# Causal mask of two attention stages: from mask products on TensorE to a minimum on VectorE

## What is computed

```python
scores = jnp.einsum('bhqk,bhsk->bhqs', q, k) / jnp.sqrt(jnp.float32(dk))
causal_mask = jnp.triu(jnp.ones((s, s), dtype=bool), k=1)
scores = jnp.where(causal_mask, jnp.float32(-1000000000.0), scores)
weights = jax.nn.softmax(scores, axis=-1)
...
num = jnp.exp(jnp.einsum('bhqd,bhkd->bhqk', q_rot, k_rot) * scale)
den = jnp.sum(jnp.exp(jnp.einsum('bhqd,bhkd->bhqk', q, k) * scale), axis=-1, keepdims=True)
attn = num / den
causal = jnp.tril(jnp.ones((C, C), dtype=bool))
attn = jnp.where(causal[None, None], attn, 0.0)
```

## Time and profile before

| | us |
|---|---|
| median of 3 runs | 5669.14 |
| lowest, highest run | 5666.31, 5673.63 |
| profiled execution, its own time | 5685.95 |
| its span in the trace | 5684.2 |

### The profile page before, as it was taken

How to read it: one execution, slowest core, us unless ns; L and a number is a source line. 1 busy time by engine, 2 the same in 40 slices (tenths; PEclk the granted TensorE clock), 3 DMA queues, 4 the chain that set the end, 5 groups by cost and what they waited for, 6 DMA issues and landing times. The chain is left out here.

```text
span 5684.2 us, 145095 instructions
## 1 busy us (share of the span) xinstructions
PE 5317.8 (94%) x51344; PEld 3675.0 (65%) x51344; DVE 3822.2 (67%) x7798; ACT 3092.0 (54%) x4722; POOL 3094.0 (54%) x1917
## 2 busy tenths in 40 slices
PE   8988967699999999999978799999999999989889
PEld 6655645377777777777755377777777777756556
DVE  2343246578877887788756487788778877855545
ACT  3343323366666666666645366666666666642542
POOL 0000014578777877787720477787778777820200
PEclk9989977799999999999979799999999999999899
DMA  1000000111111111111100111111111111110000
GB/s 41 4 1 32 1 7 2 48 37 51 45 52 44 47 49 52 44 44 52 41 15 1 38 42 52 44 47 49 52 44 43 52 43 53 36 44 1 7 23 8
DMA packets 110452, 197.68 MB, mean 35 GB/s; under 512 B 21408, under 2 KB 28848, under 8 KB 110256
## 3 DMA queue, kind: packets, MB, share of 16 engines
q1 hardware_dynamic: 110256, 194.99, 12.1%
HBM read 53.29 MB, written 1.05 MB: 10 GB/s over the span
## 5 line engine op out<-in xcount | busy, mean ns | idle before, releaser
L2660 POOL TENSOR_TENSOR stage_qk<-stage_halves 128x1024 f32<-128x1024 f32 x384 | 906.2, 2360 | 683.9 <-DVE stage_halves L2742 683.9
L2671 POOL TENSOR_TENSOR stage_rnorm<-stage_clamped,minus_half 128x16 f32<-128x16 f32 x384 | 1116.5, 2908 | 31.9
L2678 POOL TENSOR_TENSOR stage_qk<-stage_qk,stage_rnorm 128x1024 f32<-128x1024 f32 x384 | 731.2, 1904 | 15.4
L2532 ACT ACTIVATE stage_qkT<-stage_turn 128x512 f32<-128x512 f32 x768 | 457.2, 595 | 416.1 <-PE stage_turn L2270 408.0
L2512 ACT ACTIVATE stage_square<-stage_wide 128x1024 f32<-128x1024 f32 x384 | 393.5, 1025 | 417.7 <-PE stage_wide L2253 417.7
L2322 PEld LDWEIGHTS stage_pv<-stage_v_win,stage_probsT 96*64 96x64 f32 x12288 | 421.4, 137 | 303.6 <-issue 271.4
L2544 ACT ACTIVATE stage_probsT<-stage_flip 96x512 f32<-96x512 f32 x768 | 450.3, 586 | 208.6 <-PE stage_flip L2308 208.6
L2322 PE MATMUL stage_pv<-stage_v_win,stage_probsT 96*64 96x65 f32 x12288 | 528.0, 228 | 10.1 <-ACT stage_probsT L2544 8.8
L2739 DVE TENSOR_TENSOR stage_halves<-stage_wide,stage_tables 128x1024 f32<-128x1024 f32 x384 | 470.0, 1224 | 70.4 <-issue 38.0
L2742 DVE TENSOR_TENSOR stage_halves<-stage_wide,stage_tables 128x512 f32<-128x512 f32 x768 | 490.6, 680 | 0.0
L2270 PE MATMUL stage_turn<-ident,stage_qk 128*128 128x128 f32 x3072 | 478.3, 278 | 7.9 <-POOL stage_qk L2678 6.5
(11 more groups left out here) (295 smaller groups left out, 9759.7 us busy)
## 6 DMA issues: line engine op xcount, KB each, us to landing
stage_v_win<-stage_v SPq DMA_DIRECT2D x384, 195.0 KB, 2.6
stage_v_win<-stage_v SPq DMA_DIRECT2D x384, 130.0 KB, 2.4
stage_v_win<-stage_v SPq DMA_DIRECT2D x192, 65.0 KB, 2.2
stage_wq<-in_T_wq SPq DMA_DIRECT2D x12, 512.0 KB, 4.2
stage_wk<-in_T_wk SPq DMA_DIRECT2D x12, 512.0 KB, 3.4
stage_wv<-in_T_wv SPq DMA_DIRECT2D x12, 512.0 KB, 3.5
stage_wo<-in_T_wo SPq DMA_DIRECT2D x12, 512.0 KB, 3.5
stage_w_up<-in_L_w_up SPq DMA_DIRECT2D x8, 512.0 KB, 6.9
```

The lines of the kernel that those rows point to most:

```text
L2532: nc.scalar.activation(target, tiles4(turn), ACT.Copy).then_inc(att["qkT"], 1)
L2660: nc.gpsimd.tensor_tensor(qk[:, n, :], halves[:, n % 2, 0, :], halves[:, n % 2, 1, :], ALU.add)\
L2671: nc.gpsimd.tensor_tensor(rnorm[:, n, :], clamped[:, n, :], chip.minus_half[:, :].to_broadcast([P, LH]), ALU.pow)\
L2678: nc.gpsimd.tensor_tensor(heads, heads, rnorm[:, n, :].rearrange("p (h o) -> p h o", o=1).to_broadcast([P, LH, LD]), ALU.mult).then_inc(at ...
```

## The change

The eight pairs of mask products of each sample go, in level 0 and in level 3; `maskT` goes with them. The exponential is now taken of unmasked scores. For each pair VectorE takes a minimum (`keep_past`) of the diagonal blocks, 128 x 512 elements of two heads and two blocks, with a triangle `limits` that is 0 where the key is later than the query and the largest float elsewhere. `weigh` waits for the new signal `kept`, not for `probs`. The masks of level 0's `first_score` stay. `limits` adds 64 KB to each pack that the stage loads, and the load of the masks shrinks by 32 KB.

```diff
 def attention_signals(level):
...
+    if level != 2:
+        per.update(kept=PAIRS)
...
+    usable = "kept" if causal else "probs"
...
+        diagonals = probs[:, :, :].rearrange("p h (b s) -> p h b s", s=P)[:, :, 0:3:2, :]
...
-                if causal:
-                    for side in range(2):
-                        nc.tensor.matmul(kinds2(duo[:, side, :])[:, :, 0:P], ident_bf[:, :],
-                                         maskT[:, :].rearrange("p (o s) -> p o s", o=1).to_broadcast([P, T, P]),
-                                         start=True, stop=False, skip_group_check=True)
...
-                                               query[:, first:SEQ], start=not causal, stop=True, skip_group_check=True)
+                                               query[:, first:SEQ], start=True, stop=True, skip_group_check=True)
...
-                pe.wait_ge(*sig("probs", step, 2 * g + 2))
+                pe.wait_ge(*sig(usable, step, 2 * g + 2))
...
+            def keep_past(step, n):
+
+                dve.wait_ge(*sig("probs", step, n + 1))
+                own = diagonals[:, 2 * n:2 * n + 2]
+                limits = tiles["limits"].rearrange("p (h t s) -> p h t s", h=1, t=1).to_broadcast([P, 2, T, P])
+                nc.vector.tensor_tensor(own, own, limits, ALU.min).then_inc(sig["kept"], 1)
...
                 if runs(s - 1):
                     reduce(s - 1, 3)
+                if causal and runs(s - 2):
+                    keep_past(s - 2, 5)
...
+                if causal and runs(s - 2):
+                    keep_past(s - 2, 6)
                 if runs(s):
                     reduce(s, 0)
+                if causal and runs(s - 2):
+                    keep_past(s - 2, 7)
+                if causal and runs(s - 1):
+                    keep_past(s - 1, 0)
                 if runs(s - 2):
                     divide(s - 2, 0)
...
                 if runs(s):
                     reduce(s, 1)
+                if causal and runs(s - 1):
+                    keep_past(s - 1, 1)
                 if runs(s - 2):
                     divide(s - 2, 1)
+                if causal and runs(s - 1):
+                    keep_past(s - 1, 2)
...
                 if runs(s + 1):
                     copy_v(s + 1)
+                if causal and runs(s - 1):
+                    keep_past(s - 1, 3)
                 if not softmax and runs(s + 1):
                     rotate(s + 1)
                 if runs(s):
                     reduce(s, 2)
+                if causal and runs(s - 1):
+                    keep_past(s - 1, 4)
```

More of the change, by code:

```diff
@@ L791 @@
 _last = [("bo", D), ("wo", D)]
-ATTN_PARTS = {0: _every + _softmax + _last, 2: [("gamma", 1), ("beta", 1)] + _every + _softmax + _last,
-              3: _every + [("wq_swap", D), ("wk_swap", D), ("rope", 2 * SEQ)] + _last}
+ATTN_PARTS = {0: _every + _softmax + [("limits", P)] + _last, 2: [("gamma", 1), ("beta", 1)] + _every + _softmax + _last,
+              3: _every + [("wq_swap", D), ("wk_swap", D), ("rope", 2 * SEQ), ("limits", P)] + _last}
 def attention_signals(level):
@@ L825, in stage_attention @@
             tiles["rope"] = tiles["rope"].rearrange("p (n s) -> p n s", n=2)
-        masks = sb("masks", [P, 3 * P], BF16)
-        ident_bf, mask, maskT = (masks[:, n * P:(n + 1) * P] for n in range(3))
+        masks = sb("masks", [P, 2 * P], BF16)
+        ident_bf, mask = (masks[:, n * P:(n + 1) * P] for n in range(2))
         wq, wk, wv, wo, bo = (tiles[n] for n in ("wq", "wk", "wv", "wo", "bo"))
@@ L2982, in attention_layout @@
     above = np.triu(np.full((P, P), MASKED, np.float32), 1)
-    a["mask"], a["maskT"] = above.astype(bf16), np.ascontiguousarray(above.T).astype(bf16)
+    a["mask"] = above.astype(bf16)
     pairs = np.arange(D) ^ 1
@@ L3015, in attention_layout @@
     a["A3_rope"] = np.stack([np.tile(t, HEADS).astype(np.float32).T for t in tables], axis=1)
+    a["A0_limits"] = a["A3_limits"] = np.where(above.T < 0, 0.0, np.finfo(np.float32).max).astype(np.float32)
     for level, parts in ATTN_PARTS.items():
         a[f"A{level}_pack"] = joined(a, f"A{level}_", parts)
-    a["masks"] = np.concatenate([a["ident_bf"], a.pop("mask"), a.pop("maskT")], axis=1)
+    a["masks"] = np.concatenate([a["ident_bf"], a.pop("mask")], axis=1)
     del a["heads_of"], a["aug_of"]
```

## The result

The changed kernel is slower: a median of 5720.76 us (5703.44 to 5723.12, 4 runs) against 5671.39 us (5666.31 to 5673.67, 4 runs) for the kernel before on the same chip, ratio 1.0082 with a 95% interval of 1.0060 to 1.0103. That is 49 us by the medians and 47 by the ratio; I had forecast 17, in a range up to 5706. The profiled execution took 5722.89 us (span 5721.1), 36.9 us above that of before; the profiled execution of before was itself 14.6 us above its median.

A forecast was written before the change was run, and what follows sets the result against it. TensorE was busy for 94% of the span, and hand-written order within each stage was taken to count. Level 0 -13, level 3's order +11.5 and clock +18 gave +16.5 on 5669.1: 5686 us, range 5664 to 5706.

The forecast's parts named there:

- Mask products, 0.32 us each: TensorE, levels 0 and 3: each removed mask pair saves 0.32 us, 64 pairs at most 20.5 us per stage.
- Level 0, 13 us gained: Level 0: 20.5 us of masks less 4.7 for waits at `weigh` 3 and 2 for statistics; bounds 6 and 18.
- 2 us for the statistics: VectorE, level 0: statistics between pair 4's minimum and the maxima's reduction cost at most 1.07 us in two or three samples.
- Level 3, the stop: TensorE waits 3.1 us at `weigh` 3 because pair 7's minimum stands behind `reduce(s,0)`; a sample takes 26.34 us, not 24.03.
- Only pair 3's minimum in level 3 falls into such a product ... so I count 0.69 for all: VectorE: every minimum takes 0.69 us, upper end 1.02, though pair 3's in level 3 runs beside GpSimd's key product.
- The clock, 18 us: Level 3: TensorE's stops bring two half-clock stretches per sample, 3.26 us in each of six samples, less one existing fall.
- the walk: Level 3: one changed sample followed piece by piece from `weigh` 3 to `weigh` 3, 2.31 us lost, 13.9 in six samples.
- the ends: Level 3's two stage ends: some 16 pairs outside the six samples save half of their 5 us of mask products.
- Rival 3: Clock stays at half for most of level 3 and the end of level 0: +48 us, 5718 us; 11%.
- Rival 1: Level 3's stall comes but the clock hardly falls: -1.5 us, 5668 us (5660 to 5680); 22%.
- Rival 2: Levels 0 and 3: without masks, scores overlap with first scores, 4.3 and 2.9 us; clock stays up, 5655 us; 7%.
- Rival 4: The change does less than it says, for instance masks covered everywhere: level 0 gains 6 us at most, 5693 us.

The follow-up runs named there:

- no_min: Changed kernel without any minimum, the causal mask of the second scores left out in levels 0 and 3: 5643.27 us, ratio 0.9935 to the kernel before.
- l0_only: The change in level 0 alone, level 3 keeping its mask products as in the kernel before: 5670.32 us, ratio 0.9987 to the kernel before.
- fill: Changed kernel plus twelve bf16 products of no use ahead of `weigh` 3 in level 3: 5715.69 us, ratio 1.0052 to the kernel before.
- l0_reorder: Kernel before with minima in level 0 alone, statistics and pair 5's behind `add_output`, pair 7's ahead of the reduction: 5661.39 us, ratio 0.9953.
- mixed3: Level 0 as in `l0_reorder`; level 3 has minima for pairs 0, 1, 4, 5, mask products for the rest: 5653.91 us, 0.9957 to the kernel before.

## Why the prediction was wrong

The direction, the place and the mechanism of the stop were right; the size was not. By the prediction's own steps:

- **Mask products, 0.32 us each.** Right, rather low: in level 0 `no_min` gives 0.35 by samples at full clock and 0.37 by the stage.
- **Level 0, 13 us gained.** The profile has 8.0, `l0_only` 10.2 by its stage and 7 by its ratio. The wait at `weigh` 3 (0.8) was measured as 0.89, the samples as 23.0 and 23.9. What I put at 2 us for the statistics is there, but the wait that it makes is 0.95 us at the transpose of the maxima, for `add_output`, ahead of which pair 5's minimum and the statistics now stand together. What I left out was the clock: "I count nothing for its clock". The stage's mean is 0.86 after 0.89, and its last 71 us went at 0.86 where before they went at 0.98. From its last transpose of normed tokens on it takes 71.3 us after 71.8, though masks are gone there too; in `no_min` it takes 65.7. These windows are of the changed kernel and of the kernel before:

```profile
427.00:498.00 71.00, 55.85 (x587) 38.10 (x585) 39.41 (x87) 27.74 (x43) 1.02 (x1) 0.86 0.02 5
```

```profile
434.00:506.00 72.00, 58.73 (x648) 37.94 (x640) 25.09 (x64) 28.46 (x44) 1.02 (x1) 0.98 0.02 4
```

- **Level 3, the stop.** Right: pair 7's scores to `weigh` 3 in 6.48 us for 6.54, TensorE idle for 3.77.
- **"Only pair 3's minimum in level 3 falls into such a product ... so I count 0.69 for all".** This step failed. I took 1.02 us for the upper end because one row showed it; but there the operation had started 0.48 us before GpSimd's ended. The row was a part of the effect, not its bound. Started with GpSimd's product, the minimum took 2.33 us: `project` to pair 4's scores 7.12 us, not 5.82, in six samples 7.8 us.
- **The clock, 18 us.** Mis-sized, and from the same failure: the hold makes a second stop, 2.46 us at pair 4, so there are two falls per sample and not one. In the sample shown the half clock costs 4.1 us, not 3.26, and the stage's last stretch stays at 0.50. Of the 45.2 us in level 3 the order's two waits are by the walk 13.9 - 2.4 (the ends) + 7.8 = 19.3; the other 26, an estimate by difference, I put down to the clock, where I had 18. The ends gained nothing visible: the stage's last part, from its last transpose of normed tokens on, takes 87.5 us after 72.5.
- **The rivals.** Rival 3 gave 5718 for a clock that stays down, and 5721 was measured; that its price was near is in part luck, since its picture holds only half: the clock comes back to 1.00 in each sample, and stays down only at the stage's end. Rival 1 is refuted by `fill` and by the windows. Rival 2's overlap may be there (0.35 us for 0.32 in `no_min`), but is far too small to decide. Rival 4 is refuted by the 23.8 us of `no_min`.
- **The range.** It left out most of rival 3. With the hold in the sum (7.8 us) the forecast would have been 5694, and with its fall of the clock (another 1.63 in six samples, 10 us) 5704, still 17 short, by the clock at the stage's end and in level 0.

Left open: how a fall at the stage's start or end depends on what went before. The same code of level 0 took 211.5 us in `l0_reorder` and 204.5 in `mixed3`, at mean clocks of 0.85 and 0.91, the first in the slowest execution of its kernel and the second in the fastest. No run took the clock's fall away and left all waits as they were; `fill` comes nearest, at one of the two stops and by shortening its wait.

## What to carry to other kernels

When work moves to an engine with room, ask for each new instruction which instruction stands ahead of it in that engine's order and what waits for it: one that gates another engine goes ahead of a long reduction and behind the work that the other engine waits for sooner. Here the places alone of the same 64 instructions made 45 us in level 3. A wait of TensorE of some 2.5 us or more cost more than its length here: count the half clock behind it, and a second wait near it as another fall.

A duration that a trace shows under contention is a bound only if the overlap was whole: take its start against the other engine's end before using it as one.

## What the hardware showed beyond what I expected

- A VectorE operation of 128 x 512 elements on two SBUF operands took 0.68 us alone, and 2.33 us when it started 0.11 us after GpSimd's product of 1.90 us: it ended 0.54 us after that, in all six places, and in the earlier trace rows too. An operation of the same size with one operand in PSUM took 0.68 us beside such a product. The Trainium skill (GPSIMD Engine Reference, Specifications) says that the two engines share SBUF interfaces for such instructions; here that is not a sharing in halves but a wait for the end of the other instruction. No run here moved GpSimd's product itself.
- TensorE's clock stays at half in stretches in which it is busy: 25.86 of 30 us at 0.50 at the end of level 3, and in the first six of them for all 6.00 us. Shortly before, from 5482 to 5488, it was busy for 4.82 of 6 us and went at 1.00.
- Sixty-four minima more in level 3 (9 us of VectorE in two samples: 37.28 us for 28.25) changed the length of a sample by nothing, 24.02 us for 24.03.
